# Idle bf16 matmuls in front of TensorE's waiting steps of a decoder layer

## The chip, the cores and the metric

The kernel runs on one core of one Trainium2 chip. The metric is device time in microseconds (us). The kernel before took 300.36 us as the median of three runs (299.4 to 300.89).

## The reference

One post-norm decoder layer on 16 sequences of 64 tokens with 128 features, in fp32: a Mamba block (depthwise causal convolution, selective scan with 16 states over 256 channels), cross attention with 16 heads whose scores are squared instead of put through a softmax, and a gated feed-forward part with two hidden layers of 512. Each of the three is added to its input and normalised.

```
h = exp(d_t * A) * h + (d_t * u_t) * B_t;   y = sum_n h * C_t      # 16 states, 64 steps
out = ((scan + D*xc) * silu(zm)) @ W_out_i * sigmoid(z) @ W_out_o
x = layernorm(x + out)
attn = (qn @ kn.T)**2;   x = layernorm(x + (attn @ v) @ Wo.T)
h = silu(x@w1.T*s1) * (x@w2.T*s2);  h = gelu(h@h1.T*..);  h = gelu(h@h2.T*..)
x = layernorm(x + h @ w3.T * s3)
```

## The kernel before, in words

Features lie on the partitions, tokens on the free axis. The 1024 tokens are cut into four blocks (`BLOCKS`) of 256 tokens (`T`). Every block goes through five lanes: front, gates, kv, attn and ffn. In between stands the selective scan of 32 steps (8 for a block, two states each): GpSimd multiplies the input in (L1032), VectorE scans (L915), GpSimd multiplies with C (L1041), and after four steps VectorE sums over the states (`reduce`, L922, some 7.2 us each, two for a block).

`schedule()` sorts all steps of all blocks by places from hand-written tables. Each engine issues its own list in that order and never departs from it. TensorE's step functions are what the change touches. In the attn lane they are `mamba_y` (L523, L525), `gate_out` (L535), `proj_out` (L540, L544), `norm_var` (L551), `query` (L556), `query_norm` (L561), `attend` (L575), `attend_out` (L591) and `attn_out` (L599, L602). In the ffn lane they are `gate_up` (L609, four parts), `hid1` and `hid2` (`hid_layer`, L619, four parts each) and `down` (L626, L629). In the kv lane they are `keys`, `key_norm` and `values`.

All results of TensorE go through four PSUM banks in turn (`WORK_BANKS`). A step first waits until the reader of the tile four places back has emptied the bank (`wait_bank_free`), then for its own input (`wait_emptied` of an earlier tile, or another semaphore), and then multiplies. Every fp32 matmul shows as two matmul records and two weight loads in the trace.

At its start the kernel already runs 18 bf16 matmuls of 128x256 on a zero tile `mid` (L393), while the first weights are on their way.

Of the kernel before, what the change touches and what calls it, by code (L numbers as in the profile page):

```python
# [12 lines left out]
P = 128  # L13
# [39 lines left out]
def columns(parts):  # L53
    at, n = {}, 0
    for name, w in parts:
# [46 lines left out]
REDUCE_PLACE = 5.2  # L102
FETCH_PLACES = {"bc_store": -9.4, "b_fetch": -9, "c_fetch": -9, "store": 34}
ONCE_PLACES = {"prep": -23.5, "prep2": -13.5, "centre_w": 0.2, "centre_b": 2.6}
LATER = {"pe": {"values": 0.25, "query": -0.25, "mamba_y": -0.75, "keys": -0.75, "gate_up": -0.75, "bc": -0.75},
         "act": {"gate_up": -0.75, "soft": -0.25, "keys": -1, "gate_m": 0.25, "xm": 0.5, "delta": -0.25},
         "dve": {"attend_out": -0.5, "mamba_y": -0.25, "key_norm": -0.5, "norm_apply": -0.5, "gate_up": -0.5, "bc": -0.5, "values": 0.25, "soft": -0.25},
# [58 lines left out]
def decoder_layer(nc, xT, ctxT, mats, vecs, bv, cw, scratch, out):  # L166
# [10 lines left out]
    with ExitStack() as ctx:  # L177
# [204 lines left out]
        def _(pe):  # L382
            mm = nc.tensor.matmul

            def wait_mats(*names):
                for n in names:
                    pe.wait_ge(loaded[n], 16)

            def prep():
                pe.wait_ge(zeroed, 1)  # L390

                for n in range(WARM_UP):
                    mm(bank[WORK_BANKS - 1][:, 0:T], mid[:, 0:P], mid[:, :], start=True, stop=True)  # L393
                wait_mats("win_xT")
                wxT, wi = m("win_xT").rearrange("p (k n) -> p k n", k=CH), m("win_i").rearrange("p (k n) -> p k n", k=CH)
                for k in range(CH):
                    i = mm(tile(("wfx",))[:, 0:INNER], wxT[:, k, :], wi[:, k, 0:INNER], start=(k == 0), stop=(k == CH - 1))
                i.then_inc(filled, 1)
                pe.wait_ge(loaded["vec"], 16)
                bias(("bf",), 0)  # L400
                for k in range(CH):
                    i = mm(tile(("bfr",))[0:TAPS - 1, 0:INNER], v("b_x")[:, k:k + 1].broadcast_to([P, TAPS - 1]), wi[:, k, 0:INNER],
                           start=(k == 0), stop=(k == CH - 1))
                i.then_inc(filled, 1)
                for k in range(CH):
                    i = mm(tile(("wfz",))[:, 0:INNER], wxT[:, k, :], wi[:, k, INNER:2 * INNER], start=(k == 0), stop=(k == CH - 1))
                i.then_inc(filled, 1)
# [87 lines left out]
            def keys(b):  # L495
                wait_mats("kv", "wkT")
                wait_bank_free(pe, ("k", b))
                mm(tile(("k", b))[:, 0:T], m("wkT"), kv[:, tok(b)], start=True, stop=True).then_inc(filled, 1)

            def key_norm(b):  # L500
                wait_bank_free(pe, ("ssk", b))
                wait_emptied(pe, ("k", b))
                for t in range(TILES):
                    i = mm(tile(("ssk", b))[:, t * HEADS:(t + 1) * HEADS], k2[:, t * P:(t + 1) * P], m("headsel"), start=True, stop=True)  # L504
                i.then_inc(filled, 1)

            def values(b):
                wait_mats("bv")
                wait_bank_free(pe, ("v", b))
                for t in range(TILES):  # L510
                    o = tile(("v", b))[:, t * P:(t + 1) * P]
                    mm(o, kv[:, b * T + t * P:b * T + (t + 1) * P], m("wvT"), start=True, stop=False)
                    i = mm(o, ones[0:1, :], bv_row[0:1, :], start=False, stop=True)
                i.then_inc(filled, 1)

            def mamba_y(b):
                wait_bank_free(pe, ("y", b))
                pe.wait_ge(reduced, GROUPS * (b + 1))
                if b == 0:
                    pe.wait_ge(small, 6)  # L520
# [7 lines left out]
            def gate_out(b):  # L528
                wait_mats("wouti")
                wait_bank_free(pe, ("oi", b))  # L530
                wait_emptied(pe, ("y", b))
                w = m("wouti").rearrange("p (k n) -> p k n", k=CH)
                for c in range(CH):
# [3 lines left out]

            def proj_out(b):
                wait_bank_free(pe, ("d1", b))
                mm(tile(("d1", b))[:, 0:T], m("centre"), x[:, tok(b)], start=True, stop=False)  # L540
                wait_emptied(pe, ("oi", b))
                wait_emptied(pe, ("wc",))
# [4 lines left out]
            def norm_var(b, i_):  # L547
                k = norm_kind(i_)
                wait_bank_free(pe, ("var", b, i_))
                pe.wait_ge(sq_ready[k], norm_number(b, i_))  # L550
                mm(tile(("var", b, i_))[:, 0:T], mean, sq[k][:, :], start=True, stop=True).then_inc(filled, 1)  # L551

            def query(b):
                wait_bank_free(pe, ("q", b))
                wait_emptied(pe, ("d1", b))
                mm(tile(("q", b))[:, 0:T], m("wqT"), x1[:, :], start=True, stop=True).then_inc(filled, 1)  # L556

            def query_norm(b):
                wait_bank_free(pe, ("ssq", b))
                wait_emptied(pe, ("q", b))  # L560
                mm(tile(("ssq", b))[:, 0:T], m("headblk"), q2[:, :], start=True, stop=True).then_inc(filled, 1)  # L561

            def attend(b, h):
                if h == 0:
                    pe.wait_ge(qm_ready, b + 1)
                    pe.wait_ge(k_ready, b + 1)
                two = (2 * h, 2 * h + 1)
                for g in two:
                    wait_bank_free(pe, ("s", b, g))
                for p in range(PAIRS):  # L570
                    for e in range(2):
                        t = (2 * p + e) * SEQ
# [7 lines left out]
            def attend_out(b):  # L580
                for e in range(2):
                    wait_bank_free(pe, ("o", b, e))
                wait_emptied(pe, ("v", b))
                for g in range(HG):
                    wait_emptied(pe, ("s", b, g))
# [10 lines left out]

            def attn_out(b):
                wait_bank_free(pe, ("d2", b))
                mm(tile(("d2", b))[:, 0:T], ident, x1[:, :], start=True, stop=False)  # L599
                wait_emptied(pe, ("o", b, 1))  # L600
                wait_emptied(pe, ("wc",))
# [1 line left out]

            def gate_up(b, j):
                wait_mats("w1T")
                wait_emptied(pe, ("d2", b))
                wait_bank_free(pe, ("gu", b, j))
                for n, w in enumerate(("w1T", "w2T")):
                    i = mm(tile(("gu", b, j))[:, n * T:(n + 1) * T], m(w)[:, j * P:(j + 1) * P], x2[b % 2][:, :], start=True, stop=True)  # L609
                i.then_inc(filled, 1)  # L610

            def hid_layer(key, w, src, before):
                w = m(w).rearrange("p (k n) -> p k n", k=FT)

                def part_(b, j):
                    wait_bank_free(pe, (key, b, j))
                    for k in range(FT):
                        wait_emptied(pe, (before, b, k))
                        i = mm(tile((key, b, j))[:, 0:T], w[:, k, j * P:(j + 1) * P], src[:, k, :], start=(k == 0), stop=(k == FT - 1))  # L619
# [2 lines left out]

            def down(b):
                wait_bank_free(pe, ("d3", b))
                wait_emptied(pe, ("w3c",))
                mm(tile(("d3", b))[:, 0:T], ident, x2[b % 2][:, :], start=True, stop=False)  # L626
                for k in range(FT):
# [8 lines left out]
                        "gate_up": gate_up, "hid1": hid_layer("h1", "h1T", hid_a, "gu"),  # L636
                        "hid2": hid_layer("h2", "h2T", hid_b, "h1"), "down": down}
# [473 lines left out]
```

## Time and profile before

| | |
|---|---|
| median of three runs | 300.36 us |
| profiled execution | 302.26 us, span 300.5 us |
| TensorE matmul busy | 221.8 us (74%), 1426 records |
| VectorE, ScalarE, GpSimd busy | 179.4, 169.1, 164.7 us |
| mean granted TensorE clock | 0.80 of full speed |
| chain that ended last | TensorE 50%, VectorE 17%, issue 13%, GpSimd 10%, ScalarE 8% |

The profile is one execution. The span is cut into 40 slices of 7.5 us in the page's second part. The clock row there says how much of TensorE's full clock was granted; the trace knows two levels, 1.0 (2.4 GHz) and 0.5 (1.2 GHz), and values between them are slices with both. The chain is followed back from the last instruction, at each step to what released it.

### The profile page before, as it was taken

Reading aid. Unit: us, or ns where it says so; the run is one execution under the profiler, and the core shown is the slowest. Engines: PE = TensorE matmul, PEld = TensorE weight load, DVE = VectorE, ACT = ScalarE, POOL = GpSimd, SP = SyncE. Lnnn points to the kernel's source line nnn. Section 1 sums busy time; section 2 is a strip of 40 time slices with the busy share of each in tenths; the row PEclk is TensorE's granted clock in tenths of the full one; section 3 lists DMA queues with packets and bytes.
Section 4 is the critical chain, followed back from the end, with each engine's and each line's share of the span. In section 5 each row is a group of like instructions: output and inputs, shape, how many; then the busy total and the mean of one; then the engine's idle time right before and its main releaser. Section 6 shows DMA issues by size and latency. Waiting matters only on the chain.

```text
span 300.5 us, 3849 instructions
## 1 busy us (share of the span) xinstructions
PE 221.8 (74%) x1426; PEld 164.6 (55%) x1426; DVE 179.4 (60%) x159; ACT 169.1 (56%) x332; POOL 164.7 (55%) x80
## 2 busy tenths in 40 slices
PE   8997254054794649969995599897367999787993
PEld 5775242043462328848654377585245777455782
DVE  1236777979568977992568779994932930212200
ACT  3169949087078436888776569578234313714224
POOL 3006999999963999867059698698532000000000
PEclk9999557559596557999999569799655999955998
DMA  7969330443107021420005404200000000000000
GB/s 242 430 274 314 129 135 14 135 141 140 70 7 207 4 87 67 129 71 0 0 6 187 165 0 140 87 2 1 19 2 0 0 2 0 21 2 0 0 0 17
DMA packets 6980, 24.38 MB, mean 81 GB/s; under 512 B 945, under 2 KB 1714, under 8 KB 6834
## 3 DMA queue, kind: packets, MB, share of 16 engines
q1 hardware_dynamic: 6962, 24.14, 23.4%
q8 instruction: 11, 0.18, 0.3%
q14 instruction: 7, 0.06, 0.1%
HBM read 23.48 MB, written 0.66 MB: 80 GB/s over the span
## 4 chain that ended last, share of the span: by engine, by line
PE 50%; DVE 17%; issue 13%; POOL 10%; ACT 8%; DMA 1%; DVEq 0%; ACTq 0%; POOLq 0%
PE work L619 12%; DVE part L922 9%; PE work L609 7%; POOL state L1032 6%; PE work L436 4%; PE work L523 4%; POOL state L1041 3%; DVE state L915 3%; PE work L551 2%; PE work L535 2%; PE work L629 2%; PE work L525 1%; DMA mat<-mats 1%; PE work L602 1%; PE work L591 1%
## 5 line engine op out<-in xcount | busy, mean ns | idle before, releaser
L1032 POOL TENSOR_TENSOR state<-du,b_buf 128x1024 f32<-128x1024 f32 x32 | 75.2, 2352 | 26.9 <-DVE du L314 22.0
L1041 POOL TENSOR_TENSOR state<-state,c_buf 128x1024 f32<-128x1024 f32 x32 | 75.7, 2366 | 12.8 <-DVE state L915 12.8
L915 DVE TENSOR_TENSOR_SCAN state<-decay,state 128x1024 f32<-128x1024 f32 x32 | 72.5, 2276 | 6.7 <-POOL state L1032 3.8
L745 ACT ACTIVATE decay<-delta,neg_a 128x252 f32<-128x252 f32 x128 | 52.8, 462 | 15.4 <-DVE state L915 15.2
L922 DVE TENSOR_REDUCE part<-state 128x512 f32<-128x4096 f32 x8 | 57.9, 7231 | 0.0
L650 ACT ACT_TABLE_LOAD x33 | 42.3, 1283 | 1.3 <-PEq L1104 0.7
L619 PE MATMUL work<-hid_a,mat 128*128 128x256 f32 x128 | 29.1, 383 | 0.3 <-DVE hid_a L1004 0.3
L619 PE MATMUL work<-hid_b,mat 128*128 128x256 f32 x128 | 29.0, 380 | 0.3 <-ACT hid_b L820 0.3
L609 PE MATMUL work<-x,mat 128*128 128x256 f32 x64 | 24.2, 559 | 5.9 <-issue 5.9
L619 PEld LDWEIGHTS work<-hid_a,mat 128*128 128x128 f32 x128 | 23.9, 190 | 4.8 <-DVE hid_a L1004 1.8
L619 PEld LDWEIGHTS work<-hid_b,mat 128*128 128x128 f32 x128 | 24.2, 190 | 4.0 <-ACT hid_b L820 0.8
L609 PEld LDWEIGHTS work<-x,mat 128*128 128x128 f32 x64 | 18.6, 298 | 12.2 <-issue 8.1
L523 PE MATMUL work<-part,mat 128*128 128x512 f32 x16 | 10.9, 822 | 10.5 <-issue 6.2
L820 ACT ACTIVATE hid_c<-work,vec 128x256 f32<-128x256 f32 x16 | 7.5, 473 | 18.3 <-PE work L619 18.2
L436 PE MATMUL work<-x,wf 128*128 128x256 f32 (+3 forms) x64 | 17.3, 417 | 0.0
L322 POOL TENSOR_TENSOR qmask<-q,vec 128x1024 f32<-128x1024 f32 x3 | 5.7, 1896 | 18.5 <-ACT q L785 18.5
L812 ACT ACTIVATE up<-work,half_s 128x256 f32<-128x256 f32 x16 | 7.6, 474 | 12.9 <-PE work L609 12.9
L768 ACT ACTIVATE sq_attn<-work,b_centred 128x256 f32<-128x256 f32 x8 | 3.8, 473 | 19.4 <-PE work L602 17.5
L504 PE MATMUL work<-mat,k 128*128 128x16 f32 x16 | 3.4, 330 | 15.1 <-ACT k L757 15.1
L979 DVE SCALAR_TENSOR_TENSOR x<-work,b_centred,root_attn 128x256 f32<-128x256 f32 x8 | 3.8, 472 | 17.9 <-ACT root_attn L779 17.9
L436 PEld LDWEIGHTS work<-x,wf 128*128 128x128 f32 x64 | 13.1, 212 | 1.7
L1001 DVE SCALAR_TENSOR_TENSOR hid_a<-up,work 128x256 f32<-128x256 f32 x16 | 6.7, 421 | 11.4 <-ACT up L812 11.4
(132 smaller groups left out, 332.5 us busy)
## 6 DMA issues: line engine op xcount, KB each, us to landing
b_buf<-bc_scratch SPq DMA_DIRECT2D x16, 512.0 KB, 4.8
c_buf<-bc_scratch SPq DMA_DIRECT2D x16, 512.0 KB, 4.1
mat<-mats SPq DMA_DIRECT2D x1, 2560.0 KB, 14.2
mat<-mats SPq DMA_DIRECT2D x1, 640.0 KB, 4.3
cw_row<-cw SPq DMA_DIRECT2D x1, 512.0 KB, 5.2
x<-xT SPq DMA_DIRECT2D x1, 512.0 KB, 6.1
kv<-ctxT SPq DMA_DIRECT2D x1, 512.0 KB, 8.2
outT<-final SPq DMA_DIRECT2D x4, 128.0 KB, 1.7
```

Of the source, the lines that this page charges most:

```text
L436: mm(o[:, :, late:], wf4[:, k, c * P:(c + 1) * P], xs[:, :, 0:SEQ - late], start=(late == 0), stop=False, skip_group_check=True)
L523: mm(o[:, :], ident, part[(GROUPS * b + g) % 2][:, :], start=(g == 0), stop=False, skip_group_check=True)
L609: i = mm(tile(("gu", b, j))[:, n * T:(n + 1) * T], m(w)[:, j * P:(j + 1) * P], x2[b % 2][:, :], start=True, stop=True)
L619: i = mm(tile((key, b, j))[:, 0:T], w[:, k, j * P:(j + 1) * P], src[:, k, :], start=(k == 0), stop=(k == FT - 1))
L650: nc.scalar.preload_act_table_set(name)
L745: i = act_(decay[:, s % DA_RING, k, c, :].rearrange("p (s t) -> p s t", t=SEQ)[:, :, 1:], delta[b % KEEP][:, c, :].rearrange("p (s t) -> p ...
L812: act_(up[j % 2][:, :], tile(("gu", b, j))[:, 0:T], ACT.Tanh, scale=half_s1[:, j:j + 1]).then_inc(up_ready, 1)
L820: act_(dst[:, j, :], tile((key, b, j))[:, 0:T], ACT.Gelu, scale=v(scale)[:, j:j + 1]).then_inc(used["act"], 1)
L915: vec_.tensor_tensor_scan(h, decay[:, s % DA_RING, :, :, :].rearrange("p k c t -> p (k c t)"), h, 0.0, ALU.mult, ALU.add).then_inc(scanned, 1)
L922: vec_.tensor_reduce(part[g % 2][:, :], state[g % 2][:, :, :, :, :].rearrange("p q k c t -> p (c t) (q k)"), axis=AX.X, op=ALU.add).then_i ...
L1032: nc.gpsimd.tensor_tensor(slot(s), du[b % KEEP][:, None, :, :].broadcast_to([P, SG, CH, T]), b_buf[c % B_RING][:, states, None, :].broadca ...
L1041: nc.gpsimd.tensor_tensor(slot(s), slot(s), c_buf[c % C_RING][:, states, None, :].broadcast_to([P, SG, CH, T]), ALU.mult).then_inc(product, 1)
```

## The change

A helper `keep_warm(key, kind)` writes some bf16 matmuls of the zero tile `mid` on itself (128x256) into the PSUM tile that the step will overwrite. Sixteen kinds of step call it, behind their `wait_bank_free` and ahead of the wait for their input: nine kinds with 4 matmuls, seven with 2. That is 76 for a block and 304 in all. In `attend` the waits for the banks now stand ahead of the waits for the masked queries and the keys; in `gate_up` the wait for the bank stands ahead of the wait for its input. No other engine's code is changed.

```diff
+WARM = {"mamba_y": 4, "gate_out": 4, "proj_out": 4, "norm_var": 4, "query": 4, "query_norm": 4, "attend": 4, "attend_out": 4,
+        "attn_out": 4, "gate_up": 2, "keys": 2, "key_norm": 2, "values": 2, "hid1": 2, "hid2": 2, "down": 2}
...
+            def keep_warm(key, kind):
+
+                for _ in range(WARM[kind]):
+                    mm(tile(key)[:, 0:T], mid[:, 0:P], mid[:, :], start=True, stop=True)
...
             def proj_out(b):
                 wait_bank_free(pe, ("d1", b))
+                keep_warm(("d1", b), "proj_out")
                 mm(tile(("d1", b))[:, 0:T], m("centre"), x[:, tok(b)], start=True, stop=False)
                 wait_emptied(pe, ("oi", b))
...
             def attend(b, h):
-                if h == 0:
-                    pe.wait_ge(qm_ready, b + 1)
-                    pe.wait_ge(k_ready, b + 1)
                 two = (2 * h, 2 * h + 1)
                 for g in two:
                     wait_bank_free(pe, ("s", b, g))
+                if h == 0:
+                    keep_warm(("s", b, 0), "attend")
+                    pe.wait_ge(qm_ready, b + 1)
+                    pe.wait_ge(k_ready, b + 1)
...
             def attn_out(b):
                 wait_bank_free(pe, ("d2", b))
+                keep_warm(("d2", b), "attn_out")
                 mm(tile(("d2", b))[:, 0:T], ident, x1[:, :], start=True, stop=False)
                 wait_emptied(pe, ("o", b, 1))
...
             def gate_up(b, j):
                 wait_mats("w1T")
+                wait_bank_free(pe, ("gu", b, j))
+                keep_warm(("gu", b, j), "gate_up")
                 wait_emptied(pe, ("d2", b))
-                wait_bank_free(pe, ("gu", b, j))
...
                 def part_(b, j):
                     wait_bank_free(pe, (key, b, j))
+                    keep_warm((key, b, j), kind)
                     for k in range(FT):
                         wait_emptied(pe, (before, b, k))
```

On TensorE, from the end of the last block's `attend_out` to the end of the program (`mid` is the zero tile, L599 and L602 are `attn_out`, L551 `norm_var`, L609 `gate_up`, L619 the hidden layers, L626 and L629 `down`), there stood before:

```order
L599 MATMUL work<-x,mat 128x256
L602 MATMUL work<-heads_out,wouto_wo_c 128x256
L551 MATMUL work<-sq_attn,mat 128x256
L609 MATMUL work<-x_1,mat 128x256 x8
L619 MATMUL work<-hid_a,mat 128x256 x16
L619 MATMUL work<-hid_b,mat 128x256 x16
L626 MATMUL work<-x_1,mat 128x256
```

At the same place there now stands, with the changed kernel's line numbers (L394 is `keep_warm`, L618 and L621 `attn_out`, L565 `norm_var`, L629 `gate_up`, L640 a hidden layer; its first part is shown and the further parts follow in the same manner):

```order
L394 MATMUL work<-mid 128x256 x4
L618 MATMUL work<-x,mat 128x256
L621 MATMUL work<-heads_out,wouto_wo_c 128x256
L394 MATMUL work<-mid 128x256 x4
L565 MATMUL work<-sq_attn,mat 128x256
L394 MATMUL work<-mid 128x256 x2
L629 MATMUL work<-x_1,mat 128x256 x2
L394 MATMUL work<-mid 128x256 x2
L629 MATMUL work<-x_1,mat 128x256 x2
```

Nothing has changed places; two or four idle matmuls stand ahead of each step, and ahead of each of the four parts of `gate_up` and of both hidden layers.

In the middle of the program, where block 0's feed-forward part is followed by block 1's output projection, TensorE's list before was:

```order
L619 MATMUL work<-hid_b,mat 128x256 x12
L626 MATMUL work<-x_0,mat 128x256
L629 MATMUL work<-hid_c,w_c 128x256 x4
L535 MATMUL work<-yg,mat 128x256 x4
L551 MATMUL work<-sq_ffn,mat 128x256
```

and it is now (L547 is `gate_out`, L648 and L651 are `down`):

```order
L394 MATMUL work<-mid 128x256 x2
L640 MATMUL work<-hid_b,mat 128x256 x4
L394 MATMUL work<-mid 128x256 x2
L640 MATMUL work<-hid_b,mat 128x256 x4
L394 MATMUL work<-mid 128x256 x2
L640 MATMUL work<-hid_b,mat 128x256 x4
L394 MATMUL work<-mid 128x256 x2
L648 MATMUL work<-x_0,mat 128x256
L651 MATMUL work<-hid_c,w_c 128x256 x4
L394 MATMUL work<-mid 128x256 x4
L547 MATMUL work<-yg,mat 128x256 x4
L394 MATMUL work<-mid 128x256 x4
```

Here sixteen idle matmuls have come into a row of steps that had none.

## Rows read from the trace of the kernel before

**Rows 1.** Page: the span and the busy times by engine.
```profile
span 300.5 us, 3849 instructions
PE 221.8 (74%) x1426; PEld 164.6 (55%) x1426; DVE 179.4 (60%) x159; ACT 169.1 (56%) x332; POOL 164.7 (55%) x80
```

**Rows 2.** Page: TensorE's granted clock in 40 equal slices of the span.
```profile
PEclk9999557559596557999999569799655999955998
```

**Rows 3.** Page: the chain that ended last, by engine.
```profile
PE 50%; DVE 17%; issue 13%; POOL 10%; ACT 8%; DMA 1%; DVEq 0%; ACTq 0%; POOLq 0%
```

**Rows 4.** Stretches: window, length, busy by engine, PEclk, DMA share, GB/s.
```profile
131.20:155.50 24.30, 23.43 (x100) 17.56 (x100) 11.52 (x10) 17.75 (x34) 11.28 (x6) 1.00 0.01 4
...
191.90:195.30 3.40, 2.88 (x4) 1.36 (x5) 3.37 (x7) 1.32 (x4) 2.88 (x2) 0.51 0.39 134
196.60:208.20 11.60, 10.60 (x49) 8.71 (x48) 6.90 (x6) 8.96 (x18) 11.60 (x6) 1.00 0.01 1
212.40:232.90 20.50, 12.53 (x178) 8.98 (x179) 10.35 (x11) 6.38 (x12) 6.45 (x3) 0.50 0.02 8
...
243.10:257.40 14.30, 13.64 (x60) 10.67 (x58) 1.86 (x3) 4.54 (x8) 0.00 (x0) 1.00 0.00 1
263.60:277.20 13.60, 10.57 (x148) 7.51 (x148) 2.49 (x8) 3.73 (x7) 0.00 (x0) 0.50 0.01 1
280.20:295.10 14.90, 14.90 (x68) 12.80 (x68) 0.00 (x0) 3.79 (x8) 0.00 (x0) 1.00 0.00 0
```

**Rows 5.** Timeline of TensorE's 18 bf16 matmuls: start, length, what.
```profile
1.10 3.14 PE L393 MATMUL work<-mid 128*128 128x256 bf16 x14 [1.10 <-POOL mid L1018]
4.29 0.38 PE L393 MATMUL work<-mid 128*128 128x256 bf16 x2
4.40 0.27 PE L393 MATMUL work<-mid 128*128 128x256 bf16 x1
```

**Rows 6.** Line L393: durations in ns (min/median/max), first and last start in us.
```profile
L393 PE MATMUL work<-mid x18: 272/421/421, 1.1 to 4.4; 128*128 128x256 bf16 x18
```

**Rows 7.** Chain in order of time: start, length, engine and line.
```profile
77.17 3.75 PE work L523 x4
...
112.02 5.16 PE work L609 x12
...
131.22 1.96 PE work L523 x4
...
141.37 1.73 PE work L535 x8
...
145.76 0.67 PE work L551 x2
...
192.43 3.34 PE work L523 x4
```

**Rows 8.** Timeline: start, length, what, idle time before and its releaser.
```profile
121.79 2.35 POOL L1041 TENSOR_TENSOR state<-state,c_buf 128x1024 f32<-128x1024 f32 x1 [0.83 <-DVE state L915]
153.52 1.90 POOL L322 TENSOR_TENSOR qmask<-q,vec 128x1024 f32<-128x1024 f32 x1 [13.01 <-ACT q L785]
207.82 0.48 DVE L979 SCALAR_TENSOR_TENSOR x<-work,b_centred,root_attn 128x256 f32<-128x256 f32 x1 [3.56 <-ACT root_attn L779]
216.00 2.22 PE L575 MATMUL work<-qmask,keys 32*64 32x256 f32 x32 [4.24 <-DVE final L970]
222.46 0.49 DVE L993 TENSOR_TENSOR heads_out<-work,rq 128x128 f32<-128x128 f32 x2 [4.52 <-PE work L591]
225.00 1.19 PE L551 MATMUL work<-sq_attn,mat 128*128 128x256 f32 x2 [0.66 <-ACT sq_attn L768]
227.83 6.13 PE L609 MATMUL work<-x,mat 128*128 128x256 f32 x16 [1.64 <-issue]
230.88 0.48 DVE L1004 SCALAR_TENSOR_TENSOR hid_a<-work,half_s,hid_a 128x256 f32<-128x256 f32 x1
235.36 7.23 DVE L922 TENSOR_REDUCE part<-state 128x512 f32<-128x4096 f32 x1
```

More of the change, by code:

```diff
@@ L497, in keys @@
                 wait_bank_free(pe, ("k", b))
+                keep_warm(("k", b), "keys")
                 mm(tile(("k", b))[:, 0:T], m("wkT"), kv[:, tok(b)], start=True, stop=True).then_inc(filled, 1)
@@ L501, in key_norm @@
                 wait_bank_free(pe, ("ssk", b))
+                keep_warm(("ssk", b), "key_norm")
                 wait_emptied(pe, ("k", b))
@@ L509, in values @@
                 wait_bank_free(pe, ("v", b))
+                keep_warm(("v", b), "values")
                 for t in range(TILES):
@@ L517, in mamba_y @@
                 wait_bank_free(pe, ("y", b))
+                keep_warm(("y", b), "mamba_y")
                 pe.wait_ge(reduced, GROUPS * (b + 1))
@@ L530, in gate_out @@
                 wait_bank_free(pe, ("oi", b))
+                keep_warm(("oi", b), "gate_out")
                 wait_emptied(pe, ("y", b))
@@ L549, in norm_var @@
                 wait_bank_free(pe, ("var", b, i_))
+                keep_warm(("var", b, i_), "norm_var")
                 pe.wait_ge(sq_ready[k], norm_number(b, i_))
@@ L554, in query @@
                 wait_bank_free(pe, ("q", b))
+                keep_warm(("q", b), "query")
                 wait_emptied(pe, ("d1", b))
@@ L559, in query_norm @@
                 wait_bank_free(pe, ("ssq", b))
+                keep_warm(("ssq", b), "query_norm")
                 wait_emptied(pe, ("q", b))
@@ L582, in attend_out @@
                     wait_bank_free(pe, ("o", b, e))
+                keep_warm(("o", b, 0), "attend_out")
                 wait_emptied(pe, ("v", b))
@@ L610, in gate_up, with hid_layer @@
                 i.then_inc(filled, 1)
-            def hid_layer(key, w, src, before):
+            def hid_layer(kind, key, w, src, before):
                 w = m(w).rearrange("p (k n) -> p k n", k=FT)
@@ L624, in down @@
                 wait_bank_free(pe, ("d3", b))
+                keep_warm(("d3", b), "down")
                 wait_emptied(pe, ("w3c",))
@@ L635, in _ @@
                         "query_norm": query_norm, "attend": attend, "attend_out": attend_out, "attn_out": attn_out,
-                        "gate_up": gate_up, "hid1": hid_layer("h1", "h1T", hid_a, "gu"),
-                        "hid2": hid_layer("h2", "h2T", hid_b, "h1"), "down": down}
+                        "gate_up": gate_up, "hid1": hid_layer("hid1", "h1", "h1T", hid_a, "gu"),
+                        "hid2": hid_layer("hid2", "h2", "h2T", hid_b, "h1"), "down": down}
             for kind, *at in steps["pe"]:
```

## Prediction

> **What bounds the kernel now.** I read the page first: no engine is busy for the whole span [rows 1], TensorE's granted clock goes up and down through the program [rows 2], and half of the chain that ended last is TensorE's work [rows 3]. So the question is where in the program TensorE sets the pace, and at which clock. I then cut the span at the changes of the clock [rows 4]. Two sorts of stretch come out. In the first TensorE is full and at full clock: 23.43 of 24.30 us from 131.2, 10.60 of 11.60 from 196.6, 13.64 of 14.30 from 243.1, 14.90 of 14.90 from 280.2. In the second it waits for short steps of other engines and runs at half clock (0.50): 12.53 of 20.50 us from 212.4, 10.57 of 13.60 from 263.6. In a stretch of the first sort an idle matmul can only cost. In the second it may lie in a wait, and may bring the clock back sooner.
>
> The rest is the scan on VectorE and GpSimd. It isn't independent of TensorE: GpSimd stands 13.01 us for a query that TensorE delivers late, VectorE 3.56 us for block 2's norm and 4.52 us for its attention output [rows 8]. A delay of TensorE in those places is a delay of the scan.
>
> **Price of one idle matmul.** The same instruction opens the kernel. 14 of them took 3.14 us, and one record is 0.42 us long [rows 6], so one started every (3.14 − 0.42)/13 = 0.21 us [rows 5]. At the end the starts lie 4.40 − 4.29 = 0.11 us apart [rows 5]. I read the first as half and the second as full clock. An fp32 record of the same width costs 1.73/8 = 0.216 us at full clock and 5.16/12 = 0.43 us at half [rows 7], so 0.11 and 0.21 fit half of that. A group of four costs 0.44 or 0.85 us, a group of two 0.22 or 0.43 us. Bounds for one at full clock: 0.11 us if its weight load hides behind its neighbour, 0.21 us if it doesn't. I take 0.11.
>
> The Trainium skill ("TensorE: Matmul & The Clock Gate", "Measured speedup vs the span model") says that a weight load runs beside a matmul in flight only when the row groups differ. All of the idle matmuls use all rows, so by that rule each would cost its load as well, nearly twice my price, and the loss would be nearly twice what I forecast. This trace speaks against it: from 280.2 us on, 68 loads of 12.80 us lie inside 14.90 us of matmuls [rows 4].
>
> **The sum, part by part.** The time of the profiled execution is 302.26 us for a span of 300.5; the median of the runs is 300.36, and I add the difference to that median.
>
> Fills in full stretches, at full clock:
> - 82.6 to 90 us: `gate_out` and `proj_out` of block 0 follow work without a gap, 8 × 0.11 = 0.9 us.
> - 131.2 to 155.5 us: hid2 three parts (6), `down` (2), `gate_out` (4), two `norm_var` (8), `proj_out` (4), `values` (2), `query` (4), `query_norm` (4) are 34, 3.7 us. The second `norm_var` has a gap like the 0.66 us one of [rows 8], which hides 0.44; another 0.16 us gap hides part of one group. That leaves 3.1 us, and the 13.01 us wait of GpSimd passes it on.
> - 196.6 to 208.2 us: hid2 (6), `gate_out` (4), `proj_out` (4), 14 × 0.11 = 1.5 us, passed on by VectorE's 3.56 us wait.
> - 235.4 to 243.1 us: block 2's hidden layers (8) and `mamba_y` (4). The reduce beside them ends at 235.36 + 7.23 = 242.59, so it has 0.5 us less to do than TensorE and TensorE decides already: 12 × 0.11 = 1.3 us.
> - 243.1 to 257.4 us: hid2 three parts (6), `gate_out`, `proj_out`, `query` (12), `down` (2), 20 × 0.11 = 2.2 us; `norm_var` is hidden.
> - 257.4 to 265.2 us: `attend` (4) waits for its bank, so its fills begin only when the wait is over; with `values` (2) and the second `norm_var` in part, 0.8 us.
> - 280.2 to 297 us: hidden layers (7 of 8 groups) and `down`, 16 × 0.11 = 1.75 us. Nothing hides them.
>
> Fills in stretches at half clock:
> - `norm_var` in blocks 0 to 2: 0.85 us in a 0.66 us gap, 0.2 us each, 0.6.
> - `attn_out` in block 1 and block 2: the step starts behind other work or a bank wait, 0.85 each, 1.7.
> - `attend` of block 2: its 4.24 us wait is for VectorE's `final`, which empties the bank [rows 8]. The fills stand behind that wait, so the wait stays as idle as it was and 0.85 us comes on top.
>
> The fills of `attend_out`, of `gate_up`'s first part (in 1.64 us) and of `mamba_y` in blocks 0 to 2 are covered by waits. The sum of the costs is 0.9 + 3.1 + 1.5 + 1.3 + 2.2 + 0.8 + 1.75 + 0.6 + 1.7 + 0.85 = 14.7 us.
>
> **What the clock may give back.** `gate_up` runs at half clock in all four blocks. Sixteen records at 0.43 are 6.9 us and at 0.216 are 3.5. Behind them VectorE needs about 0.9 us for each part (a record of 0.48 us and its twin), so 2.3 us come back at most, less six fills of 0.11: 1.7 us. Should the clock stay low, the fills cost 6 × 0.21 = 1.3 us instead. In blocks 2 and 3 I give the high clock 55%: there TensorE now has work almost without a gap from `attn_out` on. That gives 0.55 × −1.7 + 0.45 × 1.0 = −0.5 for each. In blocks 0 and 1 GpSimd's gap of 0.83 us caps the gain [rows 8]; at 40%, 0.4 × −0.8 + 0.6 × 1.0 = +0.3 each. `mamba_y` of block 2 took 3.34 us at half clock against 1.96 for block 1's [rows 7]; the clock fell just before it, and fills of `values` and `key_norm` may hold it. Its four records would save 1.4 and the `d_skip` part some 0.2; I take half, −0.8. In block 3 `attend_out` to `norm_var` would gain some 1.9 us at full clock (0.5 for the norm alone, 1.19 against 0.67 [rows 7, 8]) and lose 1.2 at half: at even odds −0.4. Together −1.0 + 0.6 − 0.8 − 0.4 = −1.6.
>
> Costs and gains make +13.1 us. A sum over one trace counts each delay in full, while some will meet waits that the delays before them have made longer, so I take 3.1 off: +10.0 us. That is 312.3 us for a profiled execution and 310.4 us for the median.
>
> **The rivals.**
> - Full clock almost everywhere after the start (faster). Place: the waiting stretches of blocks 2 and 3 and the steps before `gate_up` in blocks 0 and 1. Price: the costs at full clock are 0.9 + 3.1 + 1.5 + 1.3 + 2.2 + 0.8 + 1.75 + 0.44 = 12.0. Gains: `gate_up` 0.8 + 0.8 + 1.7 + 1.7 = 5.0, `attend_out` to `norm_var` 1.9 in two blocks and 0.9 in the others, 5.6, and the two half-clock `mamba_y` steps 1.4 and 2.6 (3.75 against 1.96 us [rows 7], and four more records at 0.21): 14.6. The net is −2.6, 297.8 us. It decides from the point at which the gains of the clock pass 12 us. For it speaks that half the tail's span is at half clock; against it that the longest idle times end in a bank wait or last far longer than the 0.44 us of fills before them. Chance 0.10.
> - Gains and costs even out (within 0.5%). VectorE and GpSimd take most of the delays into waits of their own, about 4 us of the costs are left and the clock pays them back: 301 us. Against it speaks the full tail from 280.2 us. Chance 0.07.
> - The clock is not moved at all, which is the case that the change does not do what it says. The costs 14.7, `gate_up` 4 × 1.3 and block 3's 1.2 make +21, 321 us, and less as far as delays are absorbed: 316 to 321. Against it speaks that the opening matmuls of the same form ran into the full clock. Chance 0.13.
> - The forecast, some clock for most of the costs: 304 to 315 us. Chance 0.70.
>
> **The numbers.** 310.4 us; the range 300 to 318 holds the forecast, the even case and part of the third. A measurement here tells some 0.5% (1.5 us) from no change. Faster 0.10, within 0.5% 0.07, slower 0.83.
>
> **What would show it.** The last hidden layer's records should stay at 0.216 us with gaps of 0.22 us between groups of eight, and the stretch from the last `gate_up` to the end should be 1.7 us longer. The stretch that is now 131.2 to 155.5 should grow by 3 us and GpSimd's 13.01 us wait with it. The four-fill group should stand in front of block 2's `attend` behind the wait for `final`. The mean granted clock should rise from 0.80, to 0.85 or so. The forecast is wrong if `gate_up` runs at full clock in three or four blocks and the norm and attention steps too, or if fills in the full stretches don't lengthen them.

## The result, and the profile after

The changed kernel takes 303.69 us (median of four runs, 303.05 to 304.43) against 300.06 for the kernel before, measured beside it: a ratio of 1.012, interval 1.0084 to 1.0157. It is slower, as forecast, but by 3.6 us where 10 were forecast. The profiled execution took 303.05 us. Medians here and below are over all runs, ratios over those that lie within 1.5% of their kernel's fastest.

From the page of the changed kernel, the lines that answer to [rows 1 to 3], and the idle matmuls' own group:

```profile
span 301.2 us, 4394 instructions
...
PE 234.8 (78%) x1730; PEld 176.4 (59%) x1730; DVE 179.0 (59%) x159; ACT 169.4 (56%) x332; POOL 164.8 (55%) x80
...
PEclk9999757559598978999999799999999999999999
...
PE 49%; DVE 20%; POOL 12%; issue 9%; ACT 8%; DVEq 0%; ACTq 0%; POOLq 0%
...
L394 PE MATMUL work<-mid 128*128 128x256 bf16 x304 | 53.8, 284 | 19.0 <-DVE rest L924 10.8
```

The mean clock is 0.913 where it was 0.802, and after the slice with a 7 in the second half it never leaves its full level until the end. That is the rival "full clock almost everywhere", which I gave 0.10, from block 1's attention step on. In the first half the slices with 5 stay. Yet the time didn't follow that rival.

Four stretches of TensorE's time, as in [rows 4], the first and last at the same times as there, the others where their steps now lie (window, length, busy time of each engine, PEclk):

```profile
131.20:155.50 24.30, 24.17 (x126) 19.09 (x125) 10.66 (x10) 16.65 (x32) 9.05 (x5) 1.00 0.00 1
192.60:208.10 15.50, 15.34 (x75) 11.77 (x76) 11.18 (x11) 11.09 (x24) 15.38 (x7) 1.00 0.10 33
215.70:235.00 19.30, 14.97 (x225) 11.10 (x226) 11.27 (x14) 7.09 (x13) 4.71 (x2) 1.00 0.03 8
243.10:257.40 14.30, 14.17 (x75) 11.57 (x74) 1.86 (x3) 4.07 (x7) 0.00 (x0) 1.00 0.00 0
```

The third row is the stretch that stood at 0.50 in [rows 4]. The others are as full as before or fuller, and now hold idle matmuls besides.

Cut at landmarks (the starts of VectorE's reduces and of steps of blocks 2 and 3), the traces differ as follows, in us. The reduces are counted from 0, so 2 and 3 are those of block 1, 4 and 5 of block 2, 6 and 7 of block 3. The kernel before was profiled a second time (300.11 us, nearer its median than the first trace's 302.26), which shows how much its own stretches vary. "Waits only" and "placed" are experiments told below.

| from, to | before | before again | changed | forecast change | waits only | placed |
|---|---|---|---|---|---|---|
| start, reduce 2 | 99.6 | 98.2 | 99.3 | +0.9 | 99.0 | 99.0 |
| reduce 2, reduce 3 | 24.2 | 23.9 | 24.0 | +0.5 | 21.9 | 21.9 |
| reduce 3, reduce 4 | 32.2 | 32.2 | 34.6 | +3.1 | 34.6 | 32.2 |
| reduce 4, reduce 5 | 29.0 | 28.9 | 27.5 | +1.4 | 27.4 | 28.7 |
| reduce 5, reduce 6 | 23.2 | 24.8 | 22.8 | +0.7 | 23.5 | 22.3 |
| reduce 6, gate_up of block 2 | 19.6 | 19.1 | 18.7 | +1.9 | 19.0 | 16.8 |
| to mamba_y of block 3 | 15.1 | 14.4 | 14.7 | +0.8 | 12.7 | 12.7 |
| to gate_up of block 3 | 29.8 | 29.7 | 31.5 | +2.6 | 28.3 | 27.3 |
| to the end | 27.7 | 27.2 | 28.1 | +1.3 | 25.6 | 25.6 |
| span | 300.5 | 298.3 | 301.2 | +13.1 | 291.9 | 286.3 |

Of the stretches that were full before, reduce 3 to 4 grew by 2.4 us of the 3.1 forecast, and GpSimd's wait for the query in it went from 13.01 to 14.32 us. The stretch from `mamba_y` to `gate_up` grew by 1.7 of 2.6, but 1.43 of that is a stop told below, which the forecast didn't have. The three from reduce 4 to `gate_up` of block 2, in which TensorE had waited at half clock for a part or the whole, shrank. The rest moved by about a microsecond or less.

The price of an idle matmul is on the chain, in the last block's hidden layers (start, length, what):

```profile
281.81 1.73 PE work L640 x8
283.54 0.22 PE work L394 x2
283.75 1.73 PE work L640 x8
285.48 0.22 PE work L394 x2
```

Eight real records in 1.73 us as in [rows 7], then 0.22 us for two idle ones, in full.

One thing stands in the chain that no part of the forecast had. In block 3's `attend_out` (L609) TensorE stops in the middle of the step:

```profile
265.84 1.47 PE work L609 x90
267.30 1.21 issue
268.51 0.24 PE work L609
268.75 0.54 PE work L394 x4
```

The neighbouring matmuls start 1.43 us apart, and "issue" says that nothing in the profile was waited for. I looked for gaps like it in `attend_out`. There are three in the changed kernel's trace (from 165.5, 220.9 and 267.1 us, of 2.69, 1.38 and 1.43 us between starts) and none in either trace of the kernel before.

### The profile page after: what moved, and what is told of

Read it like the earlier page. It is cut to its first block, busy times and chain, and to the rows that moved or that the text cites. A ratio compares the mean times of both kernels' runs of the same rounds, so it can differ in the third digit from the quotient of the medians.

```text
span 301.2 us, 4394 instructions
## 1 busy us (share of the span) xinstructions
PE 234.8 (78%) x1730; PEld 176.4 (59%) x1730; DVE 179.0 (59%) x159; ACT 169.4 (56%) x332; POOL 164.8 (55%) x80
## 3 DMA queue, kind: packets, MB, share of 16 engines
q1 hardware_dynamic: 6962, 24.14, 22.3%
## 4 chain that ended last, share of the span: by engine, by line
PE 49%; DVE 20%; POOL 12%; issue 9%; ACT 8%; DVEq 0%; ACTq 0%; POOLq 0%
PE work L640 13%; DVE part L944 12%; POOL state L1054 8%; PE work L394 6%; PE work L629 4%; POOL state L1063 4%; DVE state L937 3%; PE work L534 3%; PE work L443 2%; PE work L547 2%; PE work L565 2%; PE work L651 2%; PE work L400 1%; PE work L472 1%; PE work L557 1%
## 5 line engine op out<-in xcount | busy, mean ns | idle before, releaser
L394 PE MATMUL work<-mid 128*128 128x256 bf16 x304 | 53.8, 284 | 19.0 <-DVE rest L924 10.8
L394 PEld LDWEIGHTS work<-mid 128*128 128x128 bf16 x304 | 29.4, 102 | 38.5 <-issue 12.4
L640 PE MATMUL work<-hid_a,mat 128*128 128x256 f32 x128 | 30.8, 381 | 0.1
L640 PE MATMUL work<-hid_b,mat 128*128 128x256 f32 x128 | 30.3, 379 | 0.0
L640 PEld LDWEIGHTS work<-hid_a,mat 128*128 128x128 f32 x128 | 22.9, 190 | 3.4 <-DVE hid_a L1026 0.9
L640 PEld LDWEIGHTS work<-hid_b,mat 128*128 128x128 f32 x128 | 23.1, 190 | 2.7
L629 PE MATMUL work<-x,mat 128*128 128x256 f32 x64 | 18.8, 421 | 4.7 <-DVE x L1001 4.7
L443 PE MATMUL work<-x,wf 128*128 128x256 f32 (+3 forms) x64 | 16.8, 409 | 0.0
L629 PEld LDWEIGHTS work<-x,mat 128*128 128x128 f32 x64 | 12.2, 212 | 7.3 <-DVE x L1001 6.0
L534 PE MATMUL work<-part,mat 128*128 128x512 f32 x16 | 9.6, 732 | 7.8 <-DVE part L944 7.7
L842 ACT ACTIVATE hid_b<-work,vec 128x256 f32<-128x256 f32 x16 | 7.2, 474 | 13.1 <-PE work L640 13.1
L992 DVE TENSOR_TENSOR final<-work,root_ffn 128x256 f32<-128x256 f32 x4 | 1.7, 421 | 20.8 <-ACT root_ffn L801 20.8
```

What stands on the lines that cost most here:

```text
L394: mm(tile(key)[:, 0:T], mid[:, 0:P], mid[:, :], start=True, stop=True)
L443: mm(o[:, :, late:], wf4[:, k, c * P:(c + 1) * P], xs[:, :, 0:SEQ - late], start=(late == 0), stop=False, skip_group_check=True)
L534: mm(o[:, :], ident, part[(GROUPS * b + g) % 2][:, :], start=(g == 0), stop=False, skip_group_check=True)
L842: act_(dst[:, j, :], tile((key, b, j))[:, 0:T], ACT.Gelu, scale=v(scale)[:, j:j + 1]).then_inc(used["act"], 1)
```

## Experiments

**Two halves of the change.** The 76 idle matmuls of a block were split into those ahead of steps at which TensorE waits (40), and those ahead of steps that follow its own work (36).

```diff
# waits only; the counts that change, the others are left out here
-"mamba_y": 4, "gate_out": 4, "proj_out": 4, "hid1": 2, "hid2": 2, "down": 2
+"mamba_y": 0, "gate_out": 0, "proj_out": 0, "hid1": 0, "hid2": 0, "down": 0
...
-                keep_warm(("gu", b, j), "gate_up")
+                if j == 0:
+                    keep_warm(("gu", b, j), "gate_up")
# full only: the other counts 0, and gate_up only for j > 0
```

> Idle matmuls stay only where TensorE waits: keys, key_norm, values, norm_var, query, query_norm, attend, attend_out, attn_out and the first part of gate_up (40 for a block); none in mamba_y, gate_out, proj_out, hid1, hid2, down and gate_up's parts 1 to 3. Theory A (a fill in a full stretch costs its 0.11 us in full, and the fills of the attention and norm steps are what holds the clock): the granted clock stays near 0.90, the 126 us stretch of full clock at the end survives, and the time falls by some 7 to 9 us against the changed kernel, to 295 to 297 us, below the kernel before. Rival B (the clock is held by the sum of all fills, those in the hidden layers included): the clock falls back to 0.80 to 0.85 and the time is 299 to 303 us. Rival C (fills in full stretches cost little, since other engines take the delay): the clock stays and the time stays at 302 to 304 us.

> The other half: idle matmuls only in mamba_y, gate_out, proj_out, hid1, hid2, down and gate_up's parts 1 to 3 (36 for a block), none elsewhere. Theory A: the granted clock is that of before (0.80 to 0.82), the costs stay: 7 to 10 us over the kernel before, 307 to 310 us. Rival B: the clock rises well above 0.82 and the time is under 305 us. Rival C: 300 to 302 us with the clock of before.

Measured: waits only 294.56 us, ratio 0.978 (0.9728 to 0.9832), clock 0.897. Full only 307.90 us, ratio 1.0231 (1.0175 to 1.0287), clock 0.845. The change is a gain of some 6.6 us and a loss of some 6.9 us in one. Theory A holds for the first half in time and mean clock, though the long stretch at full clock did not survive whole: it fell from 191.0 to 194.4 and from 214.9 to 221.7 us, and was full from there to 290.0. In the second half the clock rose more than the theory said, from 0.80 to 0.845, so full stretches that are made fuller have a part in the clock too. The sum of the halves (+0.3 us) is short of the whole (+3.6) by about 3 us. Neither half's trace has a stop in `attend_out`; the changed kernel's, below, are 2.8 us, which would be most of it. The intervals of the two halves leave the sum open by some 2 us, so this is likely and not shown.

One stretch shows what the second half gives. From reduce 3 to 4 waits only took 34.6 us, as long as the changed kernel with 16 more idle matmuls in that stretch, since its clock fell at block 1's `mamba_y` (129.6 to 133.0 us). Its chain:

```profile
128.29 2.51 PE work L533 x4
130.79 1.71 PE work L535 x4
132.50 5.47 PE work L640 x24
```

These 9.69 us were 8.02 in the kernel told last, which has 12 idle matmuls ahead of that `mamba_y` and full clock. So `mamba_y`, which I counted among the full steps, is one ahead of which fills can lie in a wait, the one for the reduce.

The page of the waits-only kernel, its clock:

```profile
PEclk9999857558689799988999989979978999999998
```

**The order of the waits alone** (all counts 0):

> No idle matmul beyond the opening ones; only the order of the waits in attend and gate_up is that of the changed kernel. All theories: the time of the kernel before within 0.5% (299 to 301.5 us), clock 0.80. If it is off by more, the moved waits have a part in the result.

Measured: 301.70 us, ratio 1.0018 (0.9985 to 1.0051), clock 0.818. The moved waits have no part in it.

**Twice the fills in the feed-forward steps** (`hid1`, `hid2`, `down`: 4 for 2):

> As the changed kernel, with twice the idle matmuls in hid1, hid2 and down (4 in place of 2 for each step, 72 more in all, some 46 of them in stretches in which TensorE sets the pace). Theory A: 46 x 0.11 = 5 us over the changed kernel, 308 to 309.5 us, clock unchanged at 0.91 to 0.93. Rival C: under 2 us over it. Rival B: the clock is high already, so the same as A.

Measured: 307.14 us, ratio 1.0182 (1.0125 to 1.024), clock 0.901: 3.5 us over the changed kernel by the medians, of 5 expected, and 0.9 us under Theory A's range. Its trace places them: the last stretch is 29.87 us long against 28.14, which is 16 × 0.108 us, and the one before block 3's `mamba_y` 15.56 against 14.69, 8 × 0.109. In the part between them (30.95 us) it has no stop, which pays 1.4 us back; its code lies elsewhere too, and its one stop is in block 1.

**Where the gain lies** (waits only, and none of it in blocks 0 and 1):

```diff
+                if key[1] < 2:
+                    return
                 for _ in range(WARM[kind]):
```

> As the waits-only kernel, with idle matmuls only in blocks 2 and 3. It tells where that kernel's gain of 6.3 us lies. Theory A: in blocks 2 and 3, where the tail runs on TensorE, two gate_up steps of 1.7 to 2.3 us and two rows of attention and norm steps; in blocks 0 and 1 the scan caps the gain at 0.8 us for each gate_up and the fills there cost about 1 us: 294 to 297 us, two thirds or more of the gain. Rival E (the gain lies in blocks 0 and 1 as much): 298 us or more.

Measured: 294.08 us, ratio 0.9764 (0.9728 to 0.9801), clock 0.862. All of the gain is in blocks 2 and 3. In the first two blocks fills raise the clock (0.862 without them, 0.897 with them) and gain nothing that outweighs their cost, though there too they lie in waits.

**Which of the waiting steps** (waits only, without `keys`, `key_norm`, `values`, `query`, `query_norm`, `attend`; 22 for a block):

> As the waits-only kernel, without the idle matmuls of keys, key_norm, values, query, query_norm and attend: those of norm_var, attend_out, attn_out and gate_up's first part stay (22 for a block). Theory A as I wrote it before the result (fills behind a bank wait or behind other work are cost alone; those from attend_out on bring the clock back): 292 to 294.5 us, at or under the waits-only kernel. Rival H (the fills of query, query_norm, attend and values are needed, so that the clock doesn't fall in the attention steps of blocks 2 and 3): clock under 0.88 and 296 us or more.

Measured: 295.53 us, ratio 0.9792 (0.9732 to 0.9853), clock 0.850. The clock is lower, as H has it, and the time is that of waits only, above A's range by the median and below H's. It was low around the attention steps of block 2 (213.7 to 227.3 us) with a stop of 1.79 us in its `attend_out`, and full for all that came after; the last three stretches are 12.7, 27.5 and 25.6 us. So the fills from `attend_out` to the first part of `gate_up` carry the gain.

**The same instructions on one row of the zero tile**, in the waits-only kernel and in the whole change:

```diff
-mm(tile(key)[:, 0:T], mid[:, 0:P], mid[:, :], start=True, stop=True)
+mm(tile(key)[:, 0:T], mid[0:1, 0:P], mid[0:1, :], start=True, stop=True)
```

> As the waits-only kernel, but each idle matmul has one row of the zero tile for both operands (1x128 weights, 1x256 moving) in place of 128: the same instructions and the same columns, a 128th of the array's rows. Rival F (it is the time in which the engine is busy that holds the clock): clock 0.90 and 294 to 296 us, as with all rows. Rival G (rows count): the clock falls back to 0.80 to 0.83 and the time is 299 to 303 us, the fills being a cost alone.

> The changed kernel with one-row idle matmuls (1x128 weights, 1x256 moving) at all 304 places: the same instructions in the same places, which in the waits-only kernel did not hold the clock (0.807, 309.05 us). It shows what the 304 cost when they give nothing back. Forecast's sum of costs with no clock moved: 14.7 us plus 5.2 for gate_up and 1.2 for block 3, so 316 to 321 us. Theory K (the cost terms were right within a fifth and only the clock term was too small): 313 to 320 us. Rival L (the costs were far too large as well, other engines hide them): under 311 us.

Measured: 309.05 us, ratio 1.0294 (1.0238 to 1.035), clock 0.807, and 343.70 us, ratio 1.1415 (1.1326 to 1.1505), clock 0.802. Rival G is right about the clock, and neither G nor F about the time. The second was meant to measure the costs alone, and it did not: both theories are far off, since such a matmul isn't as cheap as one on all rows. Its chain, in the same hidden layer as above:

```profile
316.76 1.92 PE work L640 x8
318.69 0.32 PE work L394 x2
319.01 1.92 PE work L640 x8
320.93 0.32 PE work L394 x2
```

Eight records and two idle ones take 1.92 + 0.32 = 2.24 us where they took 1.95. A pair costs 0.51 us in place of 0.22. The 15 us between waits only and its one-row version are therefore an upper bound for what the clock is worth, not its price.

**Where TensorE's code lies.** Idle matmuls were added ahead of block 0's `mamba_y`, inside a wait of 6.3 us, so that all later code of TensorE moves by 32, 72 or 16 instructions:

```diff
-                for _ in range(WARM[kind]):
+                for _ in range(20 if (kind, key[1]) == ("mamba_y", 0) else WARM[kind]):   # 40, 12
```

> The changed kernel with 20 in place of 4 idle matmuls ahead of block 0's mamba_y, where TensorE stands idle for 6.3 us anyway; the 16 more take 1.7 us of that wait. Their purpose is to move all later TensorE code by 32 instructions. In the changed kernel's trace TensorE stops inside attend_out for 2.69, 1.38 and 1.43 us (from 165.5, 220.9 and 267.1 us) for nothing that the profile shows, each time beside or just behind a 16 KB packet of the instruction queue; the kernel before and the waits-only kernel show no such stop. Theory S (TensorE waits for its code there, since attend_out at full clock goes through its 512 instructions in 1.4 us; where the code is fetched depends on its place in the program): the stops change in place or length, and if the two late ones go, the time falls by up to 2.8 us, to 301 us. Rival T (the stops are of another origin, of data or semaphores): they stay at the same matmuls with the same lengths, and the time stays at 303 to 304 us.

> The same with 40 in place of 4: 72 instructions of shift, the 36 more idle matmuls take 3.9 us of the 6.3 us wait. Theory S: other stops than in the changed kernel and than with 20; where none lies on the path, 300.5 to 301.5 us. Rival T: the same stops, 303 to 304 us.

> The changed kernel once more, on the same chip and in the same call as a third place of its code. Theory S (its code's place costs it 1.4 us in attend_out of block 2 and again in block 3): the same two late stops as in its first trace, 1.38 and 1.43 us long, and a time 2 to 3 us over the shifted kernel beside it. Rival U (the stops come and go from run to run, and the shifted kernels were faster by the phase of the clock alone): stops at other places or none, and a time within 1 us of the shifted kernel.

> The changed kernel with 12 in place of 4 idle matmuls ahead of block 0's mamba_y, a shift by 16 instructions, with 0.9 us more work in the 6.3 us wait. Theory S: whatever stops it has are the same in place and length wherever they are seen, and the stretches from block 3's mamba_y to its gate_up take 31.5 us with a stop in attend_out and 30.1 us without. Rival U: stretch and stop don't go together.

The stops in `attend_out` as the traces have them (start, and us between the starts of two neighbouring matmuls), with the stretch from block 3's `mamba_y` to its `gate_up`:

| kernel | blocks 0 and 1 | block 2 | block 3 | that stretch | ratio |
|---|---|---|---|---|---|
| changed | 165.5: 2.69 | 220.9: 1.38 | 267.1: 1.43 | 31.50 | 1.012 (1.0084 to 1.0157) |
| changed again | 165.3: 3.79 | 221.0: 2.45 | 269.4: 1.43 | 31.50 | 1.0118 (1.0046 to 1.0189) |
| 12 | 164.6: 3.04 | 220.2: 1.85 | 269.2: 0.75 | 31.71 | 1.0079 (1.004 to 1.0117) |
| 20 | none | none | none | 30.07 | 0.9994 (0.9952 to 1.0036) |
| 40 | 100.7: 2.18 | none | none | 30.07 | 0.9957 (0.9919 to 0.9995) |

The medians were 300.64 us (20), 300.02 (40), 305.34 (changed again) and 304.39 (12). The 20 and 40 were measured at another time than the other two, so they are compared by their ratios to the kernel before.

Block 3 is a clean comparison: the changed kernel, the 20 and the 40 have the same fills there and full clock, and the stretch is longer by 1.43 us, to the hundredth the stop's length, where there is one. Block 2 is not. In the 20 and the 40 the clock was at half in its attention steps (215.9 to 222.8 and 212.3 to 219.1 us), `attend_out` took 2.01 us there, and from reduce 6 to `gate_up` they need 19.1 and 19.0 us, no less than the changed kernel's 18.7 with its stop. That the stop of block 2 lies on the path is read from the chain below, and fits a kernel told later that has full clock and no stop there: 16.8 us, or 17.4 with the 0.6 us of fills that it saves, against 18.7 − 1.4 = 17.3. The stop in block 1 costs nothing visible, since TensorE then waits for VectorE's `rest` anyway (reduce 4 to 5 is 27.5 us with it and 27.4 without). About 2 us of the 20's lead is of another kind: between reduces 2 and 3 it took 21.9 us, with the clock up at `gate_up` of block 0, and the changed kernel 24.0, with the clock low from 108.6 to 115.5; 0.8 us of that it had lost before.

The other forecasts of these two runs came out in part. Of the changed kernel's second trace Theory S expected stops of 1.38 and 1.43 us; they stood in the same steps, but the one in block 2 was 2.45 us long. The 12 has stops still, with other lengths; the one in block 3 is half as long, but a drop of the clock there (267.5 to 270.9 us) took the difference. That the two medians lie within 1 us of each other is what Rival U had for a kernel without stops, so it decides nothing.

Where the stops stand settles more. I counted TensorE's matmul records from the start of the program, and looked up when the packet of the instruction queue that lies beside each stop had ended:

| kernel, block | last record before the stop | of the step's 128 | packet ends | TensorE goes on |
|---|---|---|---|---|
| changed, 1 | 839 | 121 | 166.80 | 168.16 |
| changed, 2 | 1216 | 116 | 220.85 | 222.23 |
| changed, 3 | 1593 | 127 | 267.24 | 268.52 |
| 12, block 1 | 839 | 113 | 166.27 | 167.64 |
| 12, block 2 | 1216 | 108 | 220.80 | 222.05 |
| 12, block 3 | 1593 | 119 | 268.37 | 269.91 |
| one row everywhere, 1 | 839 | 121 | 174.38 | 175.85 |
| one row everywhere, 2 | 1216 | 116 | 240.67 | 242.10 |

The changed kernel's second trace has the same three records, and the kernel with twice the feed-forward fills has its one stop of 3.08 us behind record 839 too. With 8 more matmuls ahead, the stop comes 8 records earlier in the step: it is tied to a place in TensorE's code and not to a matmul or its data. Full clock isn't needed for it, since the one-row kernel and the 12 stopped at half clock in block 2, and so did the kernel with 22 fills a block (1.79 us, behind record 1073). And in all 14 stops of these traces TensorE went on 1.25 to 1.56 us after the packet's end. Where there is no stop, the packet had come earlier: in the 20 it ended at 264.26 us and TensorE passed record 1593 at 265.90.

The chain of the kernel with 20 at the place of block 3's stop:

```profile
264.23 0.54 PE work L394 x4
264.77 0.04 issue
264.81 1.49 PE work L609 x91
266.29 0.54 PE work L394 x4
```

And TensorE's rows of the changed kernel in block 2, with the idle time in brackets:

```profile
220.84 0.23 PE L609 MATMUL work<-mat,vmask 64*32 64x64 f32 x2
222.23 0.25 PE L609 MATMUL work<-mat,vmask 64*32 64x64 f32 x2 [1.16 <-issue]
```

That it is code which TensorE waits for is the reading that fits all of this. The queue for instructions moved 14 packets of 16 KB in the changed kernel against 11 before, and TensorE's matmuls and weight loads are 3460 against 2852: a packet for some 250 of them in both. The three records of the stops lie 377 apart, which is three packets each time. The profile doesn't name the wait, so that last step is inferred, and why a packet comes early in one kernel and late in another is open: the kernel before also has packets during `attend_out` (221.57 to 222.68 us in block 2) and doesn't stop. (The step has 128 matmul records and 128 weight loads, 256 instructions, and not the 512 that I wrote ahead of these runs.)

```profile
q8 instruction: 14, 0.23, 0.3%
```

**The kernel before once more:**

> The kernel before once more, for a second trace: the first is of an execution of 302.26 us, 2 us over the median. All theories: 299.5 to 302.5 us, clock 0.80 to 0.83, the low stretches at the same steps; a difference of 1 to 2 us lies where a fall or rise of the clock comes one step earlier or later.

Measured: 300.11 us, span 298.3, clock 0.812. Its stretches are in the first table; the largest differences are in the start and at `mamba_y` of block 2, 1.4 and 1.6 us, where the clock fell or rose at another step, as expected.

**A version that beats both.** Idle matmuls only in waits, with their numbers set by step and block; `attend`'s go into a bank that is already free, ahead of the wait for the occupied one:

```diff
+WARM_AT = {("query", 1): 0, ("query", 2): 0, ("query", 3): 0, ("query_norm", 1): 0, ("attend", 1): 0, ("attend", 2): 20, ("attend", 3): 4,
+           ("values", 1): 0, ("values", 3): 0, ("attn_out", 1): 0, ("mamba_y", 0): 40, ("mamba_y", 1): 12, ("mamba_y", 2): 12}
...
+                if h == 0:
+                    wait_bank_free(pe, ("s", b, 1))
+                    keep_warm(("s", b, 1), "attend")
                 for g in two:
                     wait_bank_free(pe, ("s", b, g))
                 if h == 0:
-                    keep_warm(("s", b, 0), "attend")
```

> The kernel with idle matmuls only in waiting steps, with their numbers set by block: none where they follow other work (query of blocks 1 to 3, query_norm and attend of block 1, values of blocks 1 and 3, attn_out of block 1, the norm behind down), 40, 12 and 12 ahead of mamba_y in blocks 0 to 2, where TensorE stands for the reduce, and those of attend (20 in block 2, 4 in block 3) put into a bank that is free already, ahead of the wait for the bank that VectorE's final empties. Theory A (a fill costs where TensorE decides, the clock pays where it waits): mamba_y's steps come to full clock (2.0 us in place of 3.75, 2.5 and 3.0, and some 0.8 us of their diagonal part), attend loses 0.6 us of fills twice, other fills on the path some 1.5 us: 3 to 6 us under the waits-only kernel, 289 to 291.5 us. Rival D (GpSimd and VectorE are the bound by now): within 1.5 us of it, 293 to 296 us.

Measured: 287.98 us (286.35 to 289.47), ratio 0.9566 (0.9528 to 0.9605), clock 0.917. It is 13 us under the kernel before and a little better than Theory A's range. One part of the theory didn't come: block 0's `mamba_y` still took 3.41 us for its four records behind 40 idle matmuls, as TensorE then stood for another 2.52 us. Its page and the timeline of TensorE ahead of block 2's `attend` (L597):

```profile
PEclk9999856557979799999999958999999999999999
```

```profile
207.76 2.35 PE L397 MATMUL work<-mid 128*128 128x256 bf16 x20
211.61 1.30 PE L597 MATMUL work<-qmask,keys 32*64 32x256 f32 x32 [1.50 <-DVE final L998]
```

The same place in the changed kernel:

```profile
215.74 0.61 PE L394 MATMUL work<-mid 128*128 128x256 bf16 x4 [3.06 <-DVE final L992]
216.28 1.22 PE L592 MATMUL work<-qmask,keys 32*64 32x256 f32 x32
```

The four stand behind the wait for `final`, as forecast, and delay `attend` by 0.6 us. Twenty ahead of that wait cost nothing. The stretch from reduce 6 to `gate_up` is 16.8 us where the changed kernel's is 18.7, and reduce 3 to 4 is back at 32.2.

## Why the forecast was right and wrong

**Right: the costs in full stretches.** The changed kernel against waits only isolates them. To block 3's `mamba_y`: 14.69 − 12.70 = 2.0 us, for 18 fills that I put at 1.3 and, within the gain of `gate_up`, 0.65. From there to `gate_up`: 31.50 − 28.30 less the stop of 1.43 is 1.8 us for 16 fills, 1.76 by my price. To the end: 28.14 − 25.55 = 2.6 for 22 fills, 2.4. The page of the Trainium skill that I weighed ("TensorE: Matmul & The Clock Gate", "The mechanism") would have made a pair cost about twice 0.22 us; the chain has 0.22.

**Right by luck: the direction.** The kernel is slower by 3.6 us, of which 2.8 are stops that the forecast doesn't have. With the same fills but for those added in a wait, and without the late stops, the 20 has a ratio of 0.9994 and the 40 of 0.9957: costs and clock even out, which is the second rival, at 0.07. Without its stops the changed kernel would have some 0.8 us left, within the noise. Part of their lead is the rise of the clock in block 0, told above.

**Wrong: the step "What the clock may give back", −1.6 us.** It gave the high clock 55% in blocks 2 and 3, even odds to block 3's attention steps, and the attention and norm steps of block 2 the price of half clock. The runs showed full clock in all of these in the first trace. That is the sign of being wrong that I had named: `gate_up` at full clock in three blocks (1, 2 and 3), and the norm and attention steps of blocks 2 and 3 too. Of the +1.9 us from reduce 6 to `gate_up`, +1.4 from reduce 4 to 5 and +0.8 to `mamba_y` there came −0.3, −1.4 and +0.3 against the second trace of before, the first with a stop of 1.38 us inside. Those three alone are 5.5 us of the 10.2 between +13.1 and the +2.9 by which these two spans differ. Another 2.7 are from reduce 5 to 6 (−2.0 for +0.7), of which 1.6 is the difference between the two traces of before. In the last stretch, with 1.3 forecast, 0.9 came. What `gate_up` gives was sized rightly: the last stretch is 25.55 us in waits only against 27.2 and 27.7 before, near the 2.3 that I had called the most. What was wrong is the chance of it. In every trace with fills on all rows in the waits of blocks 2 and 3, `gate_up` of both ran at full clock. The attention steps of block 2 did not always: the clock was at half there in waits only, in the 20, the 40 and the 12, and fell for the norm in the changed kernel's second trace (224.5 to 227.9 us). What decides between the two there is open.

That step has a slip besides. For a `gate_up` that stays at half clock it puts the fills at 1.3 us and then counts 1.0. With 1.3 the term is −1.0 and the forecast 0.6 us further off.

**Wrong: the discount.** I took 3.1 us off for delays that meet longer waits. In the tail none did, as the three differences above show; ahead of it the traces of one kernel differ too much to tell. It brought the forecast nearer to the result for a reason that no run shows.

**Missing: the stops inside `attend_out`.** 2.8 us on the path in the first trace, 3.9 in the second.

**The rivals.** The clock did what the first rival said, but not its time. `mamba_y` of block 0 stayed at half clock (3.78 us in the chain, as in [rows 7]), and so did most of block 0's `gate_up`: its fills come at the start of a wait of 6 us, not along it. Take their 2.6 and 0.8 us from that rival's gains, and put the stops of 2.8 on its costs: 12.0 − 11.2 + 2.8 = +3.6 us. That it meets the measured time is in part chance, since not each of its parts was measured by itself. The rival in which the clock isn't moved is refuted by 0.913.

## What to carry to other kernels

Idle matmuls that hold TensorE's clock can pay where it waits, if its pace sets the time there (blocks 2 and 3, and not 0 and 1), and cost their full 0.11 us apiece where it doesn't wait, so place each group by the wait that it lies in; here that was the difference between 1.2% slower and 4.3% faster. A group issued behind a wait on a buffer doesn't fill that wait: give it another buffer. And compare a kernel with shifted code before its last per cent is believed: the sign of this result hung on it.

## What the runs showed of the hardware

- Idle matmuls on zeros kept the full clock through 126 us (173.5 to 299.8) in the changed kernel; in its second trace it fell once in that part, from 224.5 to 227.9 us, behind a stop of 2.45 us. With one row of the zero tile in place of 128 the same instructions left it at 0.807 and 0.802.
- Going from matmuls on 128 rows to one row and back costs 0.29 us for a pair, beyond the 0.22 us that the pair takes on all rows.
- TensorE can stop for 0.75 to 3.8 us in the middle of a step of 256 short instructions, which took 2.05 us at half clock and takes 1.5 at full. In four kernels the stops stood behind matmul record 839, 1216 or 1593, counted from the start, whatever part of the step that was; in 14 of 14 stops TensorE went on 1.25 to 1.56 us after a 16 KB packet of the instruction queue had ended. The queue moved one such packet for some 250 of TensorE's matmuls and weight loads (14 for 3460, 11 for 2852).
- The same kernel's stretches differ by up to 2 us from one execution or one small shift to the next, by where the clock rises and falls: 99.6 and 98.2 us up to reduce 2 for the kernel before, 24.0 and 21.9 from reduce 2 to 3 for the changed kernel and the 20.
